# Decoder layer on one core: cross attention, routing and shared expert joined into one stage

## Chip, cores and metric

The kernel runs on one core of a Trainium2 chip. The metric is the device time of one execution in microseconds (us). Engines are named as in the profile: PE is the matrix engine, PEld its weight load, DVE the vector engine, ACT the scalar engine, POOL the GpSimd engine, SP the queue that issues most DMAs.

## What is computed

One decoder layer on 16 sequences of 128 tokens with 256 features (x is 2048 x 256), in float32. Three blocks follow each other, each with a residual sum and a layer norm:

```
x = layernorm(x + self_attention(x))                 # 16 heads of 128, 4 key/value heads
x = layernorm(x + cross(x, ctx))                     # cross:
    A = max(|sum over the batch of (x Wh)(ctx Wh)^T * decay|, 1);  O = A (ctx Wh)
    cross = (relu(x wg) * (normalised O * gamma + beta)) wo
x = layernorm(x + ffn(x))                            # ffn:
    scores = softmax(x gate^T), 64 routes;  keep the 6 largest of a token, 0 elsewhere
    flat = kept scores in 8 groups of 8;  share = sum of a group
    soft = softmax within each group, over its nonzero entries alone
    ffn = sum over 8 experts of share_f * expert_f(x, soft_f) + shared expert(x)
```

The shared expert is silu(x Wg) * (x Wu), times Wd, with 352 inner features padded to 3 tiles of 128.

## The kernel before, in words

The program is written by hand, engine by engine: every engine has its own list of instructions, and semaphores order them. There are four stages, each a block that ends with all engines meeting and the stage's semaphores cleared (L80 to L85): `self_attention` (L88), `cross_attention` (L593), `route_and_share` (L1068) and `experts` (L1377). Most products are split in a high and a low part and made of three matmuls (`product`, L45; its matmuls are L48 to L50). `keep_busy` (L53, matmul L57) multiplies an identity matrix for no result, where PE would otherwise have nothing to do.

**Self attention** works through eight turns of two sequences. In the first turn PE makes the scores of the second group of heads (L302), turns the first probabilities (L356) and then projects the next queries.

**Cross attention** works in chunks of 512 tokens, four of them (CHUNKS). For each, PE makes the mixed values (`mix_values`, L757, matmul L763), the gates (`gates`, L767, matmul L774), turns the gated values (L800), multiplies them by wo (L816) and turns the normalised result (`turn_x2`, L778, transposes L711). DVE measures the mix (`mix_factors`, L936), multiplies gate and mix (L959), adds to the residual r (`add_output`, L967), and normalises half of its tiles (L904); ACT normalises the mix (L847) and the other half (L856), and moves the turned tiles to SBUF (L863); DVE makes their low part (L991). POOL applies gamma and beta to the mix along the tokens (`affine`, L665 and L667), splits the route weights (L692, L694) and adds high and low part of the turned x again (`whole`, L590).

**Routing and shared expert**, also per chunk: logits (L1213), softmax and top six on DVE (L1311 to L1336), the kept scores turned (L1225) and copied (L1345), regrouped by a one-hot matmul (L1232), the second softmax on DVE and ACT (L1349 to L1368), written three times side by side, turned (`soft_out`, L1202) into the banks `turned_bank` and `y_bank[1]`, copied by ACT in one instruction (L1261) and by DVE in two (L1303, L1304). The shared expert's inner part (`shared_in`, silu L1250, product L1288, high part L1256, low part on POOL L1163) and its output (`shared_out`, matmuls L48 to L50 into route_y, sum L1295) lie between. In chunk 2 POOL prepares the first expert's weights in one piece (L1153 to L1159, helpers L1038 and L1057). The stage ends after the last DMAs to `soft_dram` and of the second expert's weights have landed (L1144, L1145).

**Experts**: 8 experts by 4 chunks make 32 units, in four turns of two experts. For a unit PE makes gate and up (`gate_up`, three banks), the low-rank part of the unit before (`down_low`, L1567), and its output. ACT copies the low rows of the unit before to the front (`move_low`, L1643, instruction L1646), and PE's L1567 waits for that; then ACT makes the silu of the first tile (L1667). Once per expert ACT also writes the next expert's high weights (`weights_high`, L1654).

## Time and profile before

| what | value |
|---|---|
| three runs | 959.97 us median, 958.0 to 962.97 |
| profiled execution | 958.83 us, span from first to last instruction 957.0 us |
| mean granted clock of PE | 0.986 of full speed |
| busy share of the span | PE 93%, PEld 83%, DVE 68%, ACT 54%, POOL 39% |
| DMA | 37.99 MB, 40 GB/s over the span |
| self attention | 0 to 392.1 us |
| cross attention | 392.1 to 490.2 us |
| routing and shared expert | 490.2 to 572.5 us |
| experts and the last norm | 572.5 to 957.0 us |

A group of instructions is shown by line, engine and operation, with what it writes and reads. A row of a timeline begins with its start and its length in us from the start of the span, and in square brackets the idle time of the engine before it and what ended that. A float32 matmul is recorded as two passes.

### The profile page before, as it was taken

Reading aid. Unit: us, or ns where it says so; the run is one execution under the profiler, and the core shown is the slowest. Engines: PE = TensorE matmul, PEld = TensorE weight load, DVE = VectorE, ACT = ScalarE, POOL = GpSimd, SP = SyncE. Lnnn points to the kernel's source line nnn. Section 1 sums busy time; section 2 is a strip of 40 time slices with the busy share of each in tenths; the row PEclk is TensorE's granted clock in tenths of the full one; section 3 lists DMA queues with packets and bytes.
Section 4 is the critical chain, followed back from the end, with each engine's and each line's share of the span. In section 5 each row is a group of like instructions: output and inputs, shape, how many; then the busy total and the mean of one; then the engine's idle time right before and its main releaser. Section 6 shows DMA issues by size and latency. Waiting matters only on the chain. (4 is left out here: it accounts for less than half of the span.)

```text
span 957.0 us, 16063 instructions
## 1 busy us (share of the span) xinstructions
PE 893.1 (93%) x5722; PEld 797.4 (83%) x5722; DVE 654.1 (68%) x1345; ACT 521.2 (54%) x1230; POOL 371.0 (39%) x261
## 2 busy tenths in 40 slices
PE   5899999999999999899699888999999999999994
PEld 5799999999999998687578776888888888888884
DVE  4756565646565655557758875878887778788887
ACT  4555555646474655314434426565666565656654
POOL 0721212222131312025424424665747475656441
PEclk9999999999999999999999999999999999999997
DMA  6300000000000000400010021202111020200002
GB/s 220 103 12 23 1 22 0 22 0 22 0 22 11 0 12 1 136 1 1 1 65 7 6 75 44 92 28 86 29 79 72 37 85 26 90 24 23 23 2 88
DMA packets 16429, 37.99 MB, mean 40 GB/s; under 512 B 2048, under 2 KB 6912, under 8 KB 15232
## 3 DMA queue, kind: packets, MB, share of 16 engines
q1 hardware_dynamic: 15744, 35.29, 10.8%
q0 software_dynamic: 640, 2.10, 0.7%
q8 instruction: 28, 0.46, 0.2%
q14 instruction: 17, 0.14, 0.0%
HBM read 34.76 MB, written 2.62 MB: 39 GB/s over the span
## 5 line engine op out<-in xcount | busy, mean ns | idle before, releaser
L241 POOL TENSOR_TENSOR att_probs<-att_probs,att_share 128x512 f32<-128x512 f32 x64 | 66.5, 1041 | 191.0 <-DVE att_share L525 191.0
L1494 POOL TENSOR_TENSOR all_xT_lo<-moe_inner,all_xT_lo 128x512 fp32r<-128x512 f32 x64 | 82.7, 1292 | 87.8 <-ACT all_xT_lo L1671 84.5
L429 ACT ACTIVATE att_probs<-att_score,att_bias 128x128 f32<-128x128 f32 x256 | 90.7, 381 | 41.4 <-DVE att_bias L516 41.2
L1486 POOL TENSOR_TENSOR all_xT_hi<-moe_xe,all_xT_hi 128x1024 fp32r<-128x1024 f32 x31 | 74.5, 2405 | 64.0 <-ACT all_xT_hi L1630 63.9
L1671 ACT ACTIVATE all_xT_lo<-moe_inner 128x512 fp32r<-128x512 f32 x64 | 40.4, 631 | 85.8 <-DVE moe_inner L1742 85.8
L562 DVE SCALAR_TENSOR_TENSOR att_OT_lo<-att_mix,att_bv,att_OT_hi 128x512 fp32r<-128x512 f32 x64 | 45.8, 750 | 58.0 <-ACT att_OT_hi L467 58.0
L467 ACT ACTIVATE att_OT_hi<-att_mix,att_bv 128x512 fp32r<-128x512 f32 x64 | 43.5, 704 | 66.0 <-PE att_mix L50 66.0
L48 PE MATMUL att_proj<-att_xT_hi,att_Wq_hi 128*128 128x256 f32 x256 | 74.9, 293 | 2.1 <-DVE att_Wq_lo L490 1.3
L48 PE MATMUL att_acc<-att_Wo_hi,att_OT_hi 128*128 128x256 f32 x256 | 73.0, 285 | 1.6 <-DVE att_OT_lo L562 1.6
L50 PE MATMUL att_proj<-att_xT_hi,att_Wq_lo 128*128 128x256 f32 x256 | 72.1, 282 | 0.0
L49 PE MATMUL att_proj<-att_xT_lo,att_Wq_hi 128*128 128x256 f32 x256 | 72.0, 281 | 0.0
L49 PE MATMUL att_acc<-att_Wo_lo,att_OT_hi 128*128 128x256 f32 x256 | 72.0, 281 | 0.0
L50 PE MATMUL att_acc<-att_Wo_hi,att_OT_lo 128*128 128x256 f32 x256 | 72.0, 281 | 0.0
L302 PEld LDWEIGHTS att_score<-att_KT,att_QT 128*128 128x128 f32 x512 | 61.7, 194 | 12.2 <-issue 9.1
L302 PE MATMUL att_score<-att_KT,att_QT 128*128 128x128 f32 x512 | 64.3, 279 | 7.1 <-DVE att_QT L506 3.8
L1742 DVE TENSOR_TENSOR moe_inner<-moe_gu,moe_silu 128x512 f32<-128x512 f32 x64 | 44.0, 688 | 32.8 <-ACT moe_silu L1667 13.3
L445 ACT ACTIVATE att_PT_hi<-att_mix 128x512 fp32r<-128x512 f32 x64 | 37.9, 625 | 35.6 <-PE att_mix L356 35.4
L1704 DVE TENSOR_TENSOR moe_xe<-moe_xe,all_xT 128x512 f32<-128x512 f32 x64 | 44.3, 693 | 18.2 <-PE moe_xe L1529 17.2
L429 ACT ACTIVATION_READ_ACCUMULATOR att_probs<-att_score,att_bias 128x1 f32 x256 | 56.1, 219 | 0.0
L1752 DVE SCALAR_TENSOR_TENSOR all_r<-moe_y,moe_shares,all_r 128x256 f32<-128x256 f32 x128 | 52.8, 476 | 0.0
L48 PEld LDWEIGHTS att_proj<-att_xT_hi,att_Wq_hi 128*128 128x128 f32 x256 | 48.2, 188 | 4.0 <-ACT att_KT L419 2.4
L1667 ACT ACTIVATE moe_silu<-moe_gu 128x512 f32<-128x512 f32 x64 | 37.9, 593 | 24.1 <-PE moe_gu L50 21.1
(299 smaller groups left out, 2907.2 us busy)
## 6 DMA issues: line engine op xcount, KB each, us to landing
all_stage<-in_expert_w SPq DMA_DIRECT2D x8, 1152.0 KB, 5.1
moe_spread<-soft_dram SPq DMA_DIRECT2D x64, 128.0 KB
all_scale<-in_expert_scale SPq DMA_DIRECT2D x8, 320.0 KB, 5.3
att_xT<-in_xT SPq DMA_DIRECT2D x8, 256.0 KB, 3.1
att_stage<-in_Wq SPq DMA_DIRECT2D x4, 512.0 KB, 7.5
att_stage<-in_Wo SPq DMA_DIRECT2D x4, 512.0 KB, 6.3
att_x_tok<-in_x_tok POOLq DMA_DIRECT2D x8, 256.0 KB, 3.1
out<-all_r SPq DMA_DIRECT2D x4, 512.0 KB, 3.0
```

The lines of the kernel that those rows point to most:

```text
L48: pe.matmul(out, left.hi, right.hi, start=first, stop=False, **more)
L49: pe.matmul(out, left.hi, right.lo, start=False, stop=False, **more)
L50: return pe.matmul(out, left.lo, right.hi, start=False, stop=last, **more)
L241: pool.tensor_tensor(p3, p3, each, ALU.mult).then_inc(prob_ready, 1)
L302: mm = pe.matmul(score[b][:, h * S:(h + 1) * S], QT[j % 2][:, h * TOK + b * S:h * TOK + (b + 1) * S], KT[:, j % KV * TOK + b * S:j % KV * ...
L429: ins = act.activation(p_[:, c], score[b][:, c], ACT.Exp, bias=bias[b][:, h:h + 1], scale=SCALE, accum_out=m_[:, h:h + 1])
L562: dve.scalar_tensor_tensor(o4(OT.lo), mix[b][:, :].rearrange("p (h q) -> p h q", h=G), bv[:, j:j + 1], o4(OT.hi).bitcast(F32), ALU.add, AL ...
L1486: pool.tensor_tensor(xe[u % 2].lo[:, :], xe32[:, :], xe[u % 2].hi[:, :].bitcast(F32), ALU.subtract).then_inc(xe_lo, 1)
L1494: pool.tensor_tensor(innerT[u % 2].lo[at], inner[at], innerT[u % 2].hi[at].bitcast(F32), ALU.subtract).then_inc(inner_lo, 1)
L1704: dve.tensor_tensor(xe32[:, k * CT:(k + 1) * CT], xe_bank[:, :], xT32[:, k * B * S + c * CT:k * B * S + (c + 1) * CT], ALU.add).then_inc(x ...
L1742: dve.tensor_tensor(inner[rows, cols], up, silu[rows, cols], ALU.mult).then_inc(inner_ready, 1)
L1752: dve.scalar_tensor_tensor(here, y_bank[t // 2][:, t % 2 * D:(t % 2 + 1) * D], shares[:, e * B + at:e * B + at + 1], here, ALU.mult, ALU.a ...
```

## The change

Two stages become one, `cross_and_route`; its semaphores are cleared once, at its end. In detail:

- Cross attention: gamma and beta are applied by ACT to the turned mix (`affine`), where they stand along the partitions; the mix is turned before the gate multiplies it, the gate is made turned, and DVE's product is at once the operand of wo. POOL's `affine` and ACT's copy L875 go. The first mix factors are made for 2 + 2 tiles instead of 4, the last norm for 2 + 2. PE's order is rewritten; of the `keep_busy` calls of both stages the 14 after the key/value products stay, 8 + 14 + 14 + 10 + 8 go, 5 come. The variances get their epsilon in ACT's square root.
- Seam: the shared expert of chunk 0 and its logits start before the last two tiles of cross attention are turned.
- Routing: the second softmax takes the exponential of the kept scores straight from the bank, masks it by a comparison with 0 and doesn't subtract the maximum; the sum is kept above 0.5. The result is written once, not three times, turned into `y_bank` (last chunk: the first gate and up banks), and ACT copies it three times per half, in pieces of 32 x 512 (`soft_high`). DVE's copies L1303 and L1345 go to ACT. The order of all engines' lists is rewritten.
- The first expert's weights are loaded early, and POOL prepares them in eight pieces between the low parts of the shared expert.
- The stage no longer waits for its last DMAs; the experts' queue and POOL wait for them.
- Experts: `move_low` stands behind the first silu on ACT.
- Self attention, first turn: the next queries are projected ahead of the scores.

The diff, cut to the parts that the text speaks of:

```diff
+                    if j == 0 and weights:
+                        pe.wait_ge(w_lo, j + 5)
+                        for what in step_units(j, last):
+                            projects(what)
...
-                    if j == 0 and weights:
-                        pe.wait_ge(w_lo, j + 5)
...
-                    if j != 1:
+                    if j > 1 or j == 0 and not weights:
...
+    MIX = (range(0, 2), range(2, 4), range(4, 8), range(8, 12), range(12, 16))
+    NORM = (range(0, 4), range(4, 8), range(8, 12), range(12, 14), range(14, 16))
...
+        soft_bank = lambda c, n: (y_bank if c < CHUNKS - 1 else [gate_bank[0], up_bank[0]])[n]
...
+        def mix_of(t, h=0, n=1):
+
+            at = h * 2 * HD + t % 2 * HD
+            return bank[(6 if t // CB == 1 else 0) + t // 2 % 2][:, at:at + n * HD]
...
+            sp.wait_ge(route_lo, 1)
+            load_weights(sp, a, 0, stage, scale, expert_in)
...
+                if c == CHUNKS - 2:
+                    sp.wait_ge(expert_ready, 1)
+                    load_weights(sp, a, 1, stage, scale, expert_in)
...
+                elif n < 3:
+                    if n == 1:
+                        pool.wait_ge(out_ready, 2 * CHUNKS)
+                        pool.tensor_copy(beside(dq0)[:, :, 0], down_qa(stage))
+                    pool.tensor_copy(W0.hi[:, half(n - 1)], stage[:, half(n - 1)]).then_inc(expert_hi, 1)
+                elif n < 7:
+                    at = quarter(n - 3)
+                    pool.wait_ge(expert_hi, 2)
+                    pool.tensor_tensor(W0.lo[:, at], stage[:, at], W0.hi[:, at].bitcast(F32), ALU.subtract
...
+            for c in range(CHUNKS - 1):
+                whole_x2(c)
+            for u in range(CHUNKS * SI):
+                low_inner(u)
+                if u == 1:
+                    whole_x2(CHUNKS - 1)
+                if 2 <= u < 10:
+                    first_expert(u - 2)
...
+            def turn_mix(c):
+                for i in range(2):
+                    pe.wait_ge(y_ready, 2 * c + i + 1)
+                    if c >= 2:
...
+                    pe.wait_ge(yt_out, min(2 * (c + 1) + i + 1, 2 * CHUNKS))
...
-            gates(0, (0,))
-            pe.wait_ge(at_ready, 1)
-            mix_values(0)
-            gates(0, (1,))
-            mix_values(1)
-            keep_busy(pe, bank[4], ident, 8)
-            mix_values(2)
-            keep_busy(pe, bank[4], ident, 14)
...
+            pe.wait_ge(at_ready, 1)
+            mix_values(0)
+            mix_values(1)
+            gates(0)
+            keep_busy(pe, bank[4], ident, 5)
+            for c in range(CHUNKS):
+                turn_mix(c)
+                if c < CHUNKS - 2:
+                    mix_values(c + 2)
+                if c:
+                    turn_x2(c - 1)
+                outputs(c)
+                if c < CHUNKS - 1:
+                    gates(c + 1)
...
-            keep_busy(pe, bank[0], ident, 14)
...
+            def soft_out(c):
+                pe.wait_ge(soft2_ready, c + 1)
+                for n in range(GROUPS):
+                    if c < CHUNKS - 1:
+                        pe.wait_ge(share_added, 2 * c + n + 1)
+                    else:
+                        pe.wait_ge(inner_ready, SI * CHUNKS - 1)
+                    for t in range(TT):
+                        at = (t * GROUPS + n) * GR
+                        mm = pe.transpose(soft_bank(c, n)[0:GR, t * P:(t + 1) * P], soft2[:, at:at + GR], ident[:, :])
+                    mm.then_inc(soft_turned, 1)
...
+            shared_in(0, 0)
+            logits(0)
+            shared_in(0, 1)
...
             turn_x2(CHUNKS - 1)
-            keep_busy(pe, bank[0], ident, 10)
+            shared_in(0, 2)
+            for c in range(CHUNKS):
+                if c < CHUNKS - 1:
+                    shared_in(c + 1, 0)
+                turn_kept(c)
+                if c < CHUNKS - 1:
+                    shared_in(c + 1, 1)
+                flat(c)
+                if c == CHUNKS - 2:
+                    logits(c + 1)
+                shared_out(c)
+                if c < CHUNKS - 2:
+                    logits(c + 1)
+                if c < CHUNKS - 1:
+                    shared_in(c + 1, 2)
+                    soft_out(c)
 
...
-            keep_busy(pe, token_bank, ident, 8)
...
+            def affine(c):
+
+                if c == 0:
+                    act.wait_ge(const_in, 48)
+                for i in range(2):
+                    act.wait_ge(y_turned, 2 * c + i + 1)
+                    if c:
+                        act.wait_ge(wyt_out, 2 * (c - 1) + i + 1)
+                    for k in range(DK):
+                        at = slice(k * 2 * P, (k + 1) * 2 * P)
+                        ins = act.activation(YT[i][:, at], bank[4 + i][:, at], ACT.Identity, bias=beta[:, k:k + 1],
+                                             scale=gamma[:, k:k + 1])
+                    ins.then_inc(yt_out, 1)
...
+            for n in range(3):
+                normalise_mix(n)
             for c in range(CHUNKS):
-                for i in range(2):
-                    act.wait_ge(wyt_ready, 2 * c + i + 1)
-                    act.activation(WYT[i][:, :], bank[4 + i][:, :], ACT.Copy).then_inc(wyt_out, 1)
                 if c:
                     deviation(c - 1)
+                affine(c)
...
+            def soft_high(c):
+                for n in range(GROUPS):
+                    act.wait_ge(soft_turned, GROUPS * c + n + 1)
+                    for at in (0, 2 * GR):
+                        ins = act.activation(softT[n][at:at + GR, c * CT:(c + 1) * CT], soft_bank(c, n)[0:GR, :], ACT.Copy)
+                    if c:
+                        act.wait_ge(soft_stored, 16 * GROUPS * c)
+                    act.activation(softT32[:, n * CT:(n + 1) * CT], soft_bank(c, n)[0:GR, :], ACT.Copy
+                                   ).then_inc(softT32_ready, 1)
...
+            for c in range(CHUNKS):
+                if c < CHUNKS - 1:
+                    shared(c + 1, 0)
+                take_kept(c)
+                if c < CHUNKS - 1:
+                    shared(c + 1, 1)
+                exp2(c)
+                if c < CHUNKS - 1:
+                    exp1(c + 1)
+                    shared(c + 1, 2)
+                soft_high(c)
...
-                dve.wait_ge(top2_ready, n)
-                dve.tensor_tensor(e2_8, e2_8, wide(top2, TT * F, F), ALU.subtract).then_inc(less2_ready, 1)
-                dve.wait_ge(exp2_ready, n)
+
+                dve.scalar_tensor_tensor(e2[:, :], token_bank[:, 0:TT * FK], 0.0, e2[:, :], ALU.is_gt, ALU.mult
+                                         ).then_inc(masked_ready2, 1)
+
+            def soften(c):
+                n = c + 1
+                dve.wait_ge(masked_ready2, n)
                 dve.tensor_reduce(mass2[:, :], e2_8, AX.X, ALU.add).then_inc(mass2_ready, 1)
                 dve.wait_ge(mass2_ready, n)
+                dve.tensor_scalar(mass2[:, :], mass2[:, :], 0.5, None, ALU.max).then_inc(guard_ready, 1)
+                dve.wait_ge(guard_ready, n)
                 dve.reciprocal(part2[:, :], mass2[:, :]).then_inc(part2_ready, 1)
                 dve.wait_ge(part2_ready, n)
-                four = lambda t: t.rearrange("p (t f k) -> p t f k", t=TT * GROUPS, f=F // GROUPS)
...
-                for copy in range(3):
-                    to = soft2[:, :].rearrange("p (t n c) -> p n t c", t=TT * GROUPS, n=3)[:, copy]
-                    ins = dve.tensor_tensor(to.rearrange("p t (f k) -> p t f k", k=F), four(e2[:, :]),
-                                            four(part2[:, :]).to_broadcast([P, TT * GROUPS, F // GROUPS, F]), ALU.mult)
-                ins.then_inc(soft2_ready, 1)
-            shared_out(CHUNKS - 2)
-            for n in range(GROUPS):
...
+                dve.tensor_tensor(soft2[:, :].rearrange("p (t k) -> p t k", k=F), e2_8, wide(part2, TT * F, F), ALU.mult
+                                  ).then_inc(soft2_ready, 1)
...
+            factors_x2(CHUNKS - 1)
+            variance(CHUNKS)
+            factors_x2(CHUNKS)
+            dve.wait_ge(sentinels, 2)
+            shared(0, 0)
+            largest1(0)
+            shared(0, 1)
+            choose(0)
+            for i in range(2):
+                split_x2(2 * (CHUNKS - 1) + i)
+            shared(0, 2)
+            for c in range(CHUNKS):
+                if c < CHUNKS - 1:
+                    shared(c + 1, 0)
+                    shared(c + 1, 1)
+                largest2(c)
+                if c == CHUNKS - 2:
+                    largest1(c + 1)
+                soften(c)
+                if c == CHUNKS - 1:
+                    shared_out(c, (0,))
+                    split_soft(c)
+                    shared_out(c, (1,))
+                else:
+                    shared_out(c)
+                    if c < CHUNKS - 2:
+                        largest1(c + 1)
+                    choose(c + 1)
+                    shared(c + 1, 2)
+                    split_soft(c)
+
...
             for c in range(CHUNKS):
+                sp.wait_ge(soft_stored, 16 * GROUPS * (c + 1))
                 load_spread(0, c)
...
-                if not first:
+                if first:
+                    pool.wait_ge(expert_in, 64)
+                else:
                     pool.wait_ge(w_in, e * 32 - 32)
...
-                    if not (first and u == 0):
-                        move_low(g, u - 1)
                     for k, n in ((0, 0), (1, 2)):
                         rows, cols = FEATURES[k]
                         act.wait_ge(gu_ready, 3 * count(g, u) + n + 1)
                         act.activation(silu[rows, cols], gu[n][rows, :], ACT.Silu).then_inc(silu_ready, 1)
+                        if k == 0 and not (first and u == 0):
+                            move_low(g, u - 1)
```

## Rows read from the trace of the kernel before

**Rows 1.** Busy time by stretch: engine busy us (x instructions), granted clock, DMA share, GB/s

```profile
423.50:490.20 66.70, 55.59 (x302) 45.70 (x301) 45.69 (x142) 26.20 (x64) 25.55 (x17) 0.97 0.00 1
490.20:572.50 82.30, 74.11 (x448) 63.12 (x448) 62.01 (x156) 33.30 (x49) 28.75 (x20) 0.96 0.13 44
600.00:930.00 330.00, 327.58 (x1769) 282.77 (x1768) 265.72 (x444) 206.12 (x307) 197.23 (x122) 1.00 0.14 50
```

**Rows 2.** The same stretches, PE and PEld, for L57 (keep_busy) alone

```profile
423.50:490.20 66.70, 10.92 (x92) 10.82 (x92) 0.97 0.00 1
490.20:572.50 82.30, 1.95 (x16) 1.87 (x16) 0.96 0.13 44
```

**Rows 3.** Timeline of PE, first turn of self attention

```profile
27.96 1.13 PE L302 MATMUL att_score<-att_KT,att_QT 128*128 128x128 f32 x8 [2.52 <-ACT att_probs L429]
...
37.46 2.02 PE L302 MATMUL att_score<-att_KT,att_QT 128*128 128x128 f32 x16 [0.31 <-issue]
```

**Rows 4.** Timeline of PE, cross attention and the seam

```profile
460.99 1.22 PE L800 MATMUL cross_bank<-all_ident,cross_WY 128*128 128x128 f32 x8 [2.93 <-DVE all_xT_lo L991]
...
476.14 1.75 PE L711 MATMUL cross_bank<-all_ident,all_r 128*128 128x128 f32 x8 [2.69 <-DVE all_r L904]
...
490.29 1.97 PE L1213 MATMUL route_token<-all_w,all_xT 128*128 128x64 f32 x16 [1.04 <-PEq L85]
```

**Rows 5.** Busy time by stretch, two short ones in which the granted clock is low

```profile
30.00:32.00 2.00, 2.00 (x12) 2.00 (x11) 1.15 (x3) 0.00 (x0) 1.92 (x3) 0.50 0.57 213
476.00:480.00 4.00, 3.86 (x14) 3.46 (x15) 1.39 (x3) 1.68 (x3) 0.67 (x1) 0.57 0.00 0
```

**Rows 6.** Groups of ACT in 423.5:490.2 and 490.2:572.5: count | busy us, mean ns

```profile
L847 ACT ACTIVATE cross_Y<-cross_bank,cross_oshift,cross_orstd 128x128 f32<-128x128 f32 x32 | 11.6, 469 | 2.3 <-DVE cross_oshift L947 2.3
...
L1256 ACT ACTIVATE route_inner_hi<-route_inner 128x512 fp32r<-128x512 f32 x12 | 7.6, 632 | 18.4 <-DVE route_inner L1288 18.4
...
L1261 ACT ACTIVATE all_softT<-route_y 96x512 fp32r<-96x512 f32 x4 | 2.4, 594 | 0.6 <-PE route_y L1202 0.6
```

**Rows 7.** Timeline of PE, one chunk of routing and the longest gap

```profile
517.87 1.10 PE L1232 MATMUL route_token<-route_onehot,route_keptT 64*128 64x64 f32 x8
...
523.25 1.89 PE L1213 MATMUL route_token<-all_w,all_xT 128*128 128x64 f32 x16
524.96 0.48 PE L48 MATMUL route_gate<-all_xT_hi,all_Wroute_hi 128*128 128x512 f32 x1
...
527.80 0.60 PE L1202 MATMUL route_turned<-all_ident,route_soft 128*96 128x128 f32 x4
...
535.06 1.03 PE L1225 MATMUL route_turned<-all_ident,route_kept 128*64 128x128 f32 x4 [3.32 <-DVE all_softT L1304]
```

**Rows 8.** Timeline of DVE: first and last step of choosing six routes, ten forms between

```profile
548.93 0.41 DVE L1319 TENSOR_REDUCE route_mass<-route_e 128x4 f32<-128x256 f32 x1
...
551.62 0.42 DVE L1336 TENSOR_TENSOR route_kept<-route_soft,route_rest 128x256 f32<-128x256 f32 x1
```

**Rows 9.** Timelines of POOL and DVE around 408 us

```profile
408.12 5.33 POOL L694 TENSOR_TENSOR all_Wroute_lo<-all_w,all_Wroute_hi 128x2432 fp32r<-128x2432 f32 x1
...
406.53 7.07 DVE L904 TENSOR_SCALAR all_r<-all_r,cross_mv,cross_rstd 128x256 f32<-128x256 f32 x2
```

**Rows 10.** Waits of PE (us in total, times, longest); timelines of ACT and PE, two units

```profile
PE moe_dlow L1567 <- ACT all_xT_lo L1646: 6.0, 8, 1.9
...
627.61 0.60 ACT L1667 ACTIVATE moe_silu<-moe_gu 128x512 f32<-128x512 f32 x1
...
629.23 0.39 PE L1567 MATMUL moe_dlow<-all_xT_lo,all_dq 128*128 128x512 f32 x1
...
685.35 0.63 ACT L1646 ACTIVATE all_xT_lo<-all_xT_lo 48x512 fp32r<-48x512 f32 x1
685.88 0.58 ACT L1667 ACTIVATE moe_silu<-moe_gu 128x512 f32<-128x512 f32 x1
...
686.03 0.50 PE L1567 MATMUL moe_dlow<-all_xT_lo,all_dq 128*128 128x512 f32 x1 [0.41 <-ACT all_xT_lo L1646]
```

More of the change, by code:

```diff
@@ new lines, in cross_and_route @@
+        e2 = m.sb("e2", TT * FK)
+        mass2, part2 = m.sb("mass2", TT * F), m.sb("part2", TT * F)
+        soft2 = m.sb("soft2", TT * FK)
+        silu = [ctxT0[:, n * CT:(n + 1) * CT] for n in range(2)]
+        inner = [m.sb(f"inner{n}", CT) for n in range(2)]
+        innerT = [[m.split(f"inner{n}_{k}", CT) for k in range(SI)] for n in range(2)]
+        bank = [m.bank(f"bank{n}") for n in range(8)]
+        gate_bank, up_bank, y_bank = [bank[0], bank[2]], [bank[1], bank[3]], [bank[4], bank[5]]
@@ L652, in cross_attention @@
         omv2 = omv[:, :].rearrange("p (t s) -> p t s", s=2)
+        span = lambda tiles: slice(tiles[0], tiles[-1] + 1)
         def kv_to(n):
@@ new lines, in shared_out @@
+            def shared_out(c):
+                pe.wait_ge(inner_lo, SI * (c + 1))
+                for i in range(2):
+                    if c == 0:
+                        pe.wait_ge(turned2_lo, 2 * CHUNKS)
+                    else:
+                        pe.wait_ge(softT_lo, GROUPS * (c - 1) + i + 1)
+                    if c == CHUNKS - 1 and i:
+                        soft_out(c)
+                    for j in range(2):
+                        t = 2 * i + j
+                        for k in range(SI):
+                            mm = product(pe, y_bank[i][:, j * D:(j + 1) * D], innerT[c % 2][k][:, t * P:(t + 1) * P],
+                                         Wd[:, k * D:(k + 1) * D], first=k == 0, last=k == SI - 1)
+                    mm.then_inc(share_y, 1)
@@ L1274, in _, with split_x2 @@
+            def split_x2(u):
+                dve.wait_ge(turned2_hi, u + 1)
+                to = lambda part: pairs(part[:, :])[:, :, 2 * u * P:(2 * u + 2) * P]
+                dve.tensor_tensor(to(xT.lo), pairs(bank[4 + u % 2][:, :]), to(xT.hi).bitcast(F32), ALU.subtract
+                                  ).then_inc(turned2_lo, 1)
+            for n in range(3):
+                mix_factors(n)
             dve.wait_ge(small_in, 32)
@@ L1380, in experts @@
+def experts(nc, a, r, stats, ident, xT, xT32, softT, share_of, soft_dram, stage, scale, W0, dq0, soft_stored, expert_in):
     m = Memory(nc, "moe")
```

812 lines of the change are left out of this document (363 added, 449 removed).

## Prediction

> **What bounds the kernel now.** I read the busy time by stretch first. In the experts PE is busy for 327.6 of 330 us, so any wait added there is paid in full [rows 1]. Cross attention from its gates on is another matter: of 66.7 us PE is busy for 55.6, of which 10.9 are `keep_busy` [rows 1, 2]; 11.1 us idle and 10.9 of filling make 22 us in which PE waits for chains on DVE, ACT and POOL. In routing PE is busy for 74.1 of 82.3 us, 2.0 of them filling [rows 1, 2]: idle 8.2 us. Then I read PE's timeline for what ended these waits: low parts and norms on DVE in cross attention [rows 4], and one gap of 3.3 us in routing, where the bank of the kept scores is still being read [rows 7]. The granted clock is the third view: after a gap of 2.7 us the stretch 476 to 480 ran at 0.57, that is near the lower level of 1.2 GHz, and so did 30 to 32 us at 0.50, behind a gap of 2.5 us [rows 3 to 5]. So an idle PE costs twice, once for the gap and once for the next 3 or 4 us.
>
> **Self attention.** The projection is put into the 2.5 us gap [rows 3], so the clock should hold. But ACT's copies and exponentials come before the next scores, which start at 37.46 [rows 3]; they take as long as ever, and start sooner only by what the turned probabilities gain, about half of gap and slow clock. Bounds: nothing, and the gap with 0.5 us of clock, 3. I take the middle, -1.5.
>
> **Cross attention.** Filling: 54 multiplications of the identity go from the two stages and 5 come. Of the 10.9 us in this stretch 5/46 would remain, 1.2, so -9.7. Idle: I walked through the new order with the durations of the rows and find PE waiting four times. First for the decay-weighted scores, four small DVE steps of 0.3 to 0.4 (an estimate from the forms of rows 8) that half a gate covered: 1.5. Then for the affine copies before the first output, four less what mixing and turning cover: 1.5. Then twice for the turn of the normalised tiles in chunks 1 and 2: from the variance on, ACT makes a short root (0.2), four affine copies and two norms of 256 columns before the second transposes can start. A copy of 256 columns is an estimate of 0.52, between the 0.47 of 128 and the 0.63 of 512 columns, and each starts 0.1 before the last ends [rows 6, 10], so 0.42: with handoffs 2.5 to 2.9, of which PE's own 0.9 us of transposes and the end of its gates hide some: 2.3 and 2.0. Together 7.3 instead of 11.1: -3.8. The slow stretch 476 to 480 (0.43 of 4 us) goes: -1.7. Sum -15.2, between -8 (the idle time stays whole, and one slow stretch with it) and -18 (the four waits halved). The barrier's gap of 1.0 at the seam [rows 4] is among the 11.1. Ahead of this stretch, POOL's split of the route weights holds a pair of DVE norms for 7.07 us [rows 9]; other DMAs now stand before it on SP, so it moves, off the norms or onto more of them: between -1.6 and +1, I take -0.8, as only one pair is left to meet by then.
>
> **Routing.** The work on PE is the same. What decides is a loop from one regrouping to the next, since ACT's six copies (`soft_high`) stand ahead of the silu, and that ahead of the copy of the kept scores, which PE waits for. Per chunk: regrouping and shared output 5.4 and logits 1.7 [rows 7]; maximum and difference 0.9 (two forms like those of rows 8) and exponential 0.4; choosing 3.1 [rows 8]; product 0.7 (an estimate, 512 columns against the 0.42 of 256 in rows 8) and high part 0.63; six copies of 0.59, starting 0.1 before the last ends, as ACT's do at 685 us [rows 6, 10]: 3.0; silu 0.6, product 0.7, high part 0.6, copy of the kept scores 0.6. That is 18.3, with ten handoffs of 0.05 18.8. DVE drops nine steps a chunk (four of the softmax, two of three writes, three copies) and gains a guard; that helps, and is in the walk. The head, to the first regrouping: five inner parts of 2.8 (524.96 to 527.80 [rows 7]), logits, 1.3 of transposes and about 2.7 us of waits, 19.7. Then three periods of 18.8, the last 0.5 longer, because the logits of chunk 3 there wait 3.5 us for the mask. The tail: regrouping 1.0, exponential and mask 1.3, second softmax 1.5, turn 0.9, six copies 3.0, subtraction and sum 1.4, barrier 1.0: 10.1. Sum 86.7, less 0.9 for the transposes counted above, 85.8 instead of 82.3: +3.5. So the long gap [rows 7] goes, and the copies take its place.
>
> The waits for DMAs left out at the end are in that walk, as it ends with the last sum. The two new waits in the experts, SP's for `soft_stored` and POOL's for `expert_in`, I cost at nothing: the second weights are requested some 10 us before the stage ends, and what is queued behind the waits, the first spread on SP and the scaling on POOL, is wanted some us into the stage. Without that cover it is a late DMA, 1 to 3 us once.
>
> **POOL and clock in the joint stage.** In the rows a DVE step whose operands all lie in SBUF stands still while POOL works [rows 9]. The Trainium skill (SBUF — State Buffer, section "SBUF: two separate sides") says why: the two share one port pair as an exclusive lock, and whoever comes second blocks for the whole instruction. The trace agrees, the 7.07 us end with POOL's 5.33. By that rule the eight pieces speak against the change, as they stand where DVE chooses and softens; by it alone the sum would be some 6 us higher.
>
> From rows: a quarter of the split is about 1.3 us (5.33 by 4), a low part 1.3; I find two or three meetings on the loop, half a piece each: +1, bounds 0 and +7. The new waits of 2 to 4.5 us will lower the clock three or four times, at 1.7 each as at 476, partly off the loop: +3, bounds 0 and +17. No filling stands before the experts any more: +0.5.
>
> **Experts.** `move_low` behind the silu is free in most units: the silu starts at 627.6 and PE wants the rows at 629.23; 0.6 and 0.63 fit [rows 10]. Seven times, after ACT has written the next expert's weights, both start late: PE already waits 0.41 at 686.03, and the silu takes 0.53 more ahead of it [rows 10]. The eight waits of 6.0 us are these seven and the tail [rows 10]. Seven times 0.53: +3.7, bounds 0 and +5.
>
> **Sum.** -1.5 -0.8 -15.2 +3.5 +1 +3 +0.5 +3.7 = -5.8, from 958.8 of the profiled execution to 953.0. The median lies 1.1 higher and the runs spread over 5 us, so I leave it at 953.0. About 0.5%, 4.8 us, is what a measurement can tell from no change: faster is below 955.2, slower above 964.8.
>
> **Rivals.**
> *Clock and experts cost nothing.* The waits are too short to lower the clock, and the silu's delay is hidden: 953 - 3 - 3.7 = 946. For it: gaps of 2.9 us at 461 left the clock alone [rows 4]. Against it: the experts have no slack [rows 1]. Chance 0.20.
> *POOL meets DVE at every step.* Six meetings of whole pieces, about +6 more: 959, no difference. For it: one such meeting cost over 6 us [rows 9]; the sentence on the port lock is this case. Against it: most of DVE's steps read PSUM. Chance 0.25.
> *The clock stays low around the loop's PE part: slower.* After each wait for the copies comes PE's longest part of the loop. If the lower level holds from the regrouping through the logits, 7.1 us double after the second regrouping, 7 around the late logits of chunk 3 and 3.2 in the last chunk, 17.3 instead of 3: 967. It decides if the granted clock is under 0.6 over those whole stretches. For it: 30 to 32 and 476 to 480 [rows 5]. Against it: both ended within 4 us of steady work. Chance 0.15.
> That the edit doesn't remove the seam or the filling can't be: both are plain in the lists.
>
> **How the numbers follow.** The forecast has 0.40, with a range of its own of 949 to 957; four fifths of that count as faster. Faster: 0.32 + 0.20 + 0.03 of the 959 case = 0.55; slower: 0.15 + 0.01; the same: 0.29. The range leaves out the slower case and the edge of the first rival: 942 to 964.
>
> **What would show it.** Right: cross attention from 423 us to its last output in about 50 us; regroupings 19 us apart with PE waiting about 2 us for ACT's copy before each; the experts some 8 to 11 us earlier; waits for `move_low` of about 0.9 in seven units. Wrong: regroupings under 17 us apart (then the copies are not the loop), waits for `move_low` unchanged, or a span of the experts that differs from before by something else than about 4 us.

## The result and the profile after

The changed kernel takes 963.42 us (median of 20 runs, 960.83 to 965.25), the kernel before 960.14 us: a ratio of 1.0035, 95% interval 1.0027 to 1.0044. It is slower by 3.3 us. That is less than the 0.5% that the forecast took as the least that can be told from no change, but the interval leaves 1 out, and the 953 us that were named lie on the other side of it. The range of 942 to 964 holds it by half a microsecond. The profiled execution took 962.99 us with a span of 961.3, 4.3 more than the 957.0 before.

Busy time by stretch, changed kernel: cross attention from its first mix to its last output, then routing and shared expert up to the experts' first matmul, then the same part of the experts as in [rows 1]. Columns as there.

```profile
423.40:475.84 52.44, 44.39 (x227) 38.39 (x227) 34.67 (x123) 27.81 (x68) 6.28 (x3) 0.97 0.00 1
475.84:572.34 96.50, 77.99 (x443) 67.95 (x441) 47.38 (x140) 47.99 (x76) 29.28 (x26) 0.88 0.06 22
600.00:930.00 330.00, 324.74 (x1746) 280.01 (x1745) 263.98 (x441) 204.14 (x303) 196.52 (x121) 1.00 0.14 50
```

Cross attention went as forecast: 52.4 us instead of the 66.7 of [rows 1]. But the next stretch takes 96.5 us where routing took 82.3, and there the granted clock is 0.88 instead of 0.96. The same stretches for the filling multiplications of L57 alone:

```profile
423.40:475.84 52.44, 1.28 (x10) 1.27 (x10) 0.97 0.00 1
475.84:572.34 96.50, 0.00 (x0) 0.00 (x0) 0.88 0.06 22
```

Timeline of PE in the changed kernel: the waits over 1.2 us from the first mix to the experts, and the first regrouping (495.44). L1049 is the regrouping, L987 the logits, L1176 ACT's copy of the kept scores.

```profile
424.73 3.72 PE L910 MATMUL cross_bank<-held_V,cross_AT 128*128 128x256 f32 x16 [1.37 <-DVE cross_AT L1251]
437.44 3.72 PE L958 MATMUL cross_bank<-all_cross_w,held_turned_mix 128*128 128x256 f32 x16 [1.82 <-DVE held_turned_mix L1278]
458.90 1.33 PE L856 MATMUL cross_bank<-all_ident,all_r 128*128 128x128 f32 x8 [2.39 <-ACT all_r L1131]
471.60 1.12 PE L856 MATMUL cross_bank<-all_ident,all_r 128*128 128x128 f32 x8 [2.12 <-ACT all_r L1131]
...
495.44 1.10 PE L1049 MATMUL cross_bank<-cross_onehot,cross_keptT 64*128 64x64 f32 x8
515.38 1.97 PE L1049 MATMUL cross_bank<-cross_onehot,cross_keptT 64*128 64x64 f32 x8 [3.16 <-ACT cross_keptT L1176]
536.91 1.10 PE L1049 MATMUL cross_bank<-cross_onehot,cross_keptT 64*128 64x64 f32 x8 [2.12 <-ACT cross_keptT L1176]
541.26 3.68 PE L987 MATMUL cross_bank<-cross_Wr,all_xT 128*128 128x64 f32 x16 [3.25 <-DVE cross_e L1390]
559.66 1.97 PE L1049 MATMUL cross_bank<-cross_onehot,cross_keptT 64*128 64x64 f32 x8 [4.46 <-ACT cross_keptT L1176]
572.34 0.76 PE L1594 MATMUL moe_xe<-all_softT,all_W_hi 96*128 96x512 f32 x1 [3.66 <-PEq L85]
```

The four waits of cross attention are those of the walk (1.5, 1.5, 2.3 and 2.0 were forecast). The regroupings stand 19.9, 21.5 and 22.8 us apart, PE waits each time for ACT's copy, and the same 8 matmuls that take 1.10 us at 536.91 take 1.97 at 515.38 and 559.66, where the granted clock is low. Busy time by stretch, around the three waits of over 3 us in the loop and at the start of the experts (the third column from the right is the granted clock):

```profile
514.00:522.00 8.00, 6.62 (x33) 6.50 (x34) 3.60 (x9) 3.89 (x6) 5.24 (x4) 0.57 0.04 10
538.00:550.00 12.00, 8.75 (x48) 8.74 (x48) 3.64 (x10) 4.00 (x5) 2.11 (x3) 0.57 0.01 1
558.00:566.00 8.00, 6.34 (x31) 6.16 (x32) 3.26 (x9) 3.26 (x5) 0.00 (x0) 0.57 0.57 205
572.00:576.00 4.00, 3.66 (x16) 3.50 (x17) 1.38 (x2) 0.00 (x1) 1.72 (x2) 0.57 0.26 86
```

Near the lower level of 1.2 GHz (0.5) for most of 8, 12 and 8 us, where [rows 5] had shown stretches of 2 to 4 us. The fall in the second stretch begins at 538.1 us, just as PE goes into the wait for the mask that ends at 541.26, so it follows the wait of 2.12 us ahead of the regrouping and not only the longer one.

### The profile page after: what moved, and what is told of

Read it like the earlier page. It is cut to its first block and busy times, and to the rows that moved or that the text cites. A ratio compares the mean times of both kernels' runs of the same rounds, so it can differ in the third digit from the quotient of the medians.

```text
span 961.3 us, 15888 instructions
## 1 busy us (share of the span) xinstructions
PE 888.6 (92%) x5640; PEld 797.9 (83%) x5640; DVE 627.4 (65%) x1312; ACT 537.8 (56%) x1261; POOL 351.8 (37%) x251
## 5 line engine op out<-in xcount | busy, mean ns | idle before, releaser
L1769 DVE TENSOR_TENSOR moe_xe<-moe_xe,all_xT 128x512 f32<-128x512 f32 x64 | 44.3, 692 | 19.9 <-PE moe_xe L1594 18.9
```

The lines of the kernel that those rows point to most:

```text
L1769: dve.tensor_tensor(xe32[:, k * CT:(k + 1) * CT], xe_bank[:, :], xT32[:, k * B * S + c * CT:k * B * S + (c + 1) * CT], ALU.add).then_inc(x ...
```

## The experiments

Two questions: where the time went that the walk had saved, and whether the low clock costs anything, since slow matmuls beside a wait are free. All ratios below are to the kernel before, run on the same chip.

**The low rows ahead of the silu again.**

```diff
                 for u in range(UNITS):
+                    if not (first and u == 0):
+                        move_low(g, u - 1)
                     for k, n in ((0, 0), (1, 2)):
...
-                        if k == 0 and not (first and u == 0):
-                            move_low(g, u - 1)
```

> The changed kernel, with the copy of the low rows ahead of the first silu on ACT again, as it was before. Theory: the change of place is paid at the first unit after each write of the next expert's weights, where PE's wait grew from 0.41 to 0.87 us; seven such waits at 0.47 give 3.3 us, so about 960.1 us (0.9966 of the changed kernel). Rival: those waits are covered a little later by a fuller buffer, so PE gains less than 1 us: 962.5 to 963.4.

Measured: 959.33 us, 0.9996 (0.9982 to 1.0011). PE's waits for the low rows, first in the changed kernel, then in this one:

```profile
PE moe_dlow L1632 <- ACT all_xT_lo L1711: 9.3, 8, 2.4
```

```profile
PE moe_dlow L1632 <- ACT all_xT_lo L1711: 6.0, 8, 1.9
```

Back to the 6.0 of [rows 10]. From the experts' first matmul to the end it is 385.73 us (956.0 - 570.27) against 388.96 (961.3 - 572.34): 3.2, where 3.3 was expected.

**Filling in the loop's waits.**

```diff
+                keep_busy(pe, token_bank, ident, (0, 12, 8, 16)[c])
                 flat(c)
                 if c == CHUNKS - 2:
+                    keep_busy(pe, turned_bank, ident, 13)
                     logits(c + 1)
...
+            keep_busy(pe, token_bank, ident, 13)
```

> The changed kernel, with keep_busy in PE's waits of the routing loop: 12, 8 and 16 multiplications ahead of the regroupings of chunks 1, 2 and 3, 13 ahead of the last logits, 13 at the end of the stage; they fill 2.8, 1.9, 3.8, 3.1 and 3.1 us of waits of 3.2, 2.1, 4.5, 3.3 and 3.7. Theory: the waits themselves stay, but the granted clock holds, so PE's work behind them is not stretched: 2.7 us in the second period, 3.7 in the third, 2 in the tail and 1.6 at the start of the experts, together about 10: 953.5 us. Rival: the loop is bound by ACT and DVE alone and the slow matmuls lie beside them: under 3 us, 960.5 to 963.4, with regroupings still 20 to 23 us apart. A third: the filling itself delays PE where a wait is shorter than taken, then slower than 963.4.

Measured: 954.99 us, 0.9958 (0.9940 to 0.9975), 8.4 us less than the changed kernel by the medians and 7.4 by the ratios, though it does more work. The same stretches as above, and the regroupings:

```profile
514.00:522.00 8.00, 7.49 (x65) 7.23 (x65) 3.81 (x10) 3.89 (x6) 5.28 (x4) 1.00 0.03 8
538.00:550.00 12.00, 11.66 (x89) 10.53 (x88) 7.45 (x27) 2.99 (x5) 0.00 (x0) 1.00 0.01 1
558.00:566.00 8.00, 6.74 (x58) 6.46 (x57) 2.72 (x5) 3.41 (x6) 0.83 (x1) 1.00 0.23 88
```

```profile
495.41 1.10 PE L1049 MATMUL cross_bank<-cross_onehot,cross_keptT 64*128 64x64 f32 x8
515.38 1.10 PE L1049 MATMUL cross_bank<-cross_onehot,cross_keptT 64*128 64x64 f32 x8 [0.51 <-ACT cross_keptT L1179]
534.27 1.10 PE L1049 MATMUL cross_bank<-cross_onehot,cross_keptT 64*128 64x64 f32 x8 [0.34 <-ACT cross_keptT L1179]
553.81 1.10 PE L1049 MATMUL cross_bank<-cross_onehot,cross_keptT 64*128 64x64 f32 x8 [0.88 <-ACT cross_keptT L1179]
565.18 0.47 PE L1597 MATMUL moe_xe<-all_softT,all_W_hi 96*128 96x512 f32 x1 [1.26 <-PEq L85]
```

The second regrouping happens to stand at 515.38 in both. From there to the experts it is 49.8 us at the full clock and 57.0 in the changed kernel: 7.2 us for the clock in the loop and the tail, and 1.1 more in the experts' first units (from their first matmul to the first wait for low rows 23.7 against 24.8 us). The first period, which had the full clock in both, is 20.0 against 19.9 us. The second and third are 18.9 and 19.5 us; forecast were 18.8 and 19.3. The rival, in which the slow matmuls lie beside the chain, falls. The 7.2 are rather too low: here the experts start 1.8 us behind the end of DVE's last sum (563.39), in the changed kernel 1.3 behind it (571.05), as the filling at the end of the stage lasts longer than that sum. So the clock cost some 7.7 us (an estimate from these times).

**The last logits in the usual place.**

```diff
                 flat(c)
-                if c == CHUNKS - 2:
-                    logits(c + 1)
                 shared_out(c)
-                if c < CHUNKS - 2:
+                if c < CHUNKS - 1:
                     logits(c + 1)
...
-                if c == CHUNKS - 2:
-                    largest1(c + 1)
                 soften(c)
...
-                    if c < CHUNKS - 2:
-                        largest1(c + 1)
+                    largest1(c + 1)
                     choose(c + 1)
```

> The changed kernel, with the logits of chunk 3 behind the shared output of chunk 2 on PE, and their maximum behind its sums on DVE, as in the other chunks. Theory: the 3.3 us in which PE waits for the mask go, with most of the low clock behind it; the third period falls from 22.8 to about 20 us, the kernel to about 960 us. Rival: the period is set by ACT's and DVE's chain, and the later logits lengthen it by as much as the wait was: 963 to 965.

Measured: 960.47 us, 0.9998 (0.9983 to 1.0014). The third period fell from 22.8 to 18.4 us (536.89 to 555.31), the experts start at 568.48 instead of 572.34. PE makes the output products while it would have waited for the mask, so their sums on DVE are done (544.6) before the maximum of chunk 3 (545.68). In the changed kernel they came behind slow logits and slow output products, the last at 550.8, and the choice of chunk 3, queued behind them on DVE, began at 551.4 instead of 547.05. Part of the gain is the clock: without the wait for the mask it falls at 538.3 us all the same, behind the regrouping's wait of 2.13 us, but that fall lasts 3.4 instead of 10.2 us. What the order is worth at the full clock, the four edits below show.

**POOL's pieces later.**

```diff
-                if 2 <= u < 10:
-                    first_expert(u - 2)
+                if u >= 5:
+                    first_expert(u - 5)
+            first_expert(7)
```

> The changed kernel, with POOL's eight pieces of the first expert begun three inner parts later, so that none runs while DVE softens chunk 0. Theory: there two DVE steps took 0.79 and 0.91 instead of 0.18 and 0.43 us, and the first period of the loop shrinks by about 1.1 us from 19.9: 962.3 us, no more than the measurement can just tell. Rival (POOL meets DVE at every step): the meetings are what stretches the loop, and moving them away takes 3 us or more: under 960.5.

Measured: 959.77 us, 1.0000 (0.9982 to 1.0019): the rival's number. But the trace gives the rival only 0.9 us of it. In the changed kernel two steps of DVE and two instructions of POOL (timelines):

```profile
500.43 0.79 DVE L1398 TENSOR_SCALAR cross_mass<-cross_mass 128x32 f32<-128x32 f32 x1
...
501.64 0.91 DVE L1404 TENSOR_TENSOR cross_soft<-cross_e,cross_part 128x256 f32<-128x256 f32 x1
...
499.89 1.28 POOL L810 TENSOR_TENSOR cross_inner_lo<-cross_inner,cross_inner_hi 128x512 fp32r<-128x512 f32 x1
...
501.12 1.14 POOL L825 CAST all_W_hi<-all_stage 128x1152 fp32r<-128x1152 f32 x1
```

and the same two steps here:

```profile
500.96 0.18 DVE L1399 TENSOR_SCALAR cross_mass<-cross_mass 128x32 f32<-128x32 f32 x1
...
501.56 0.42 DVE L1405 TENSOR_TENSOR cross_soft<-cross_e,cross_part 128x256 f32<-128x256 f32 x1
```

Each of the two ended just behind a POOL instruction, and 1.1 us went there, the first period falling from 19.9 to 19.0 us. This is the lock of the forecast (the Trainium skill, SBUF — State Buffer, section "SBUF: two separate sides"), met once in the loop, not at every step. The rest is the clock: PE's wait at the second regrouping was 2.11 instead of 3.16 us, the clock did not fall behind it, and the second period took 19.0 instead of 21.5 us. That a wait of 2.1 us is short enough is not shown: behind the wait of the same length at the third regrouping of this execution the clock fell at 535.1, 1.1 us after its end, as PE went into the wait for the mask.

**The changed kernel again.**

> The changed kernel itself again, beside the three that follow, for their differences and for the clock. Theory: where the granted clock falls behind a wait of about 2 us is not the same in every execution; of the changed kernel's falls those behind the long waits of the loop (515, 541 and 560 us) are there again, those behind the short ones (378 and 460 us) need not be, and the time lies within 2 us of 963.4. Rival: the falls stand where they stood, all six.

Measured: 963.25 us, 1.0041 (1.0027 to 1.0055). The falls around the long waits are there again. Of the short ones, those at 378 and 460 are not, and others are, at 47 and 470 us. Two waits of this execution:

```profile
458.46 1.12 PE L856 MATMUL cross_bank<-all_ident,all_r 128*128 128x128 f32 x8 [2.40 <-ACT all_r L1131]
469.48 1.12 PE L856 MATMUL cross_bank<-all_ident,all_r 128*128 128x128 f32 x8 [2.12 <-ACT all_r L1131]
```

and the stretches behind them:

```profile
460.00:464.00 4.00, 4.00 (x21) 3.51 (x20) 3.39 (x7) 0.21 (x1) 2.35 (x1) 1.00 0.01 4
470.00:474.00 4.00, 4.00 (x14) 3.26 (x14) 1.34 (x3) 1.09 (x2) 1.86 (x1) 0.57 0.00 0
```

In the first profile it was the other way round, with the same two waits to 0.01 us.

**Four edits together** (low rows, logits, pieces, and filling of 8, 8 and 16 ahead of the regroupings and 13 at the end).

> The changed kernel with four edits: low rows ahead of the silu, logits of chunk 3 in the usual place, POOL's pieces three inner parts later, and keep_busy in the loop's waits (8, 8 and 16 ahead of the regroupings, 13 at the end). Theory: the kernel with filling alone took 955.0; from it go 3.3 for the low rows, 1.3 for the logits and 1.1 for the pieces: 949.3, about 0.989 of the kernel before. Rival: with the clock held the three edits were only worth what the clock gave by chance, and the time stays near 955 (952 to 956).

Measured: 946.98 us, 0.9869 (0.9853 to 0.9884), 2.3 under the sum; the edits don't only give what the clock gave. Its profile says where the rest lies: the third period is 16.8 us against 19.5 in the kernel with filling alone, so the order of the logits is worth 2.8 at the full clock, not 1.3; and the way from the start of cross attention to the first regrouping is 1.7 us shorter, with one fall of the clock less, which is no work of the edits.

**More filling, outside the loop.**

```diff
+                if c >= 2:
+                    pe.wait_ge(r_ready, 2 * (c - 1) + 1)
+                    keep_busy(pe, bank[6], ident, 8)
                 if c:
                     turn_x2(c - 1)
...
+                        if last and j == KV - 1 and b == 0:
+                            keep_busy(pe, score[0], ident, 4)
```

> The same four edits, and keep_busy in three waits more: 4 in the last turn of self attention, 8 ahead of the turned norms of chunks 1 and 2 in cross attention. Theory: those waits cost the clock in part of the executions, 1.6 us at 378 and 1.6 at 460; filled, the kernel takes 1 to 3 us less than the one with the four edits, some 947. Rival: the falls were an accident of one profiled execution, the median stays the same within 0.5; or the filling stands in the way, then up to 1 us slower.

Measured: 945.84 us, 0.9855 (0.9840 to 0.9871): 1.1 less, at the lower end, with intervals that overlap. In the profiles cross attention's last output starts 1.4 us earlier (469.19 against 470.60), and the low clock at 458 us is gone.

**The third copy by POOL.**

```diff
-                    for at in (0, 2 * GR):
-                        ins = act.activation(softT[n][at:at + GR, c * CT:(c + 1) * CT], soft_bank(c, n)[0:GR, :], ACT.Copy)
+                    act.activation(softT[n][0:GR, c * CT:(c + 1) * CT], soft_bank(c, n)[0:GR, :], ACT.Copy)
...
+            def third_copy(c):
+                for n in range(GROUPS):
+                    pool.wait_ge(softT32_ready, GROUPS * c + n + 1)
+                    cols = slice(c * CT, (c + 1) * CT)
+                    pool.tensor_copy(softT[n][2 * GR:3 * GR, cols], softT[n][0:GR, cols].bitcast(F32)).then_inc(third, 1)
+                    pool.wait_ge(third, GROUPS * c + n + 1)
```

> The last kernel, with the third copy of the turned softmax made by POOL instead of ACT (two of six copies a chunk), and filling of 3, 3, 12 and 12 instead of 8, 8, 16 and 13, as the waits get shorter. Theory: ACT's six copies lie in the loop from one regrouping to the next, so it shrinks by two of them, some 1.2 us, in each of three periods and in the tail: 4 to 5 us, about 942.5, with regroupings some 17 us apart. Rival: the loop is set by DVE's steps, whose two subtractions follow the copies anyway: under 1.5 us. A third: POOL's copies (some 1 us each) get in the way of the low parts, and nothing is gained.

Measured: 941.04 us, 0.9810 (0.9796 to 0.9823), 4.8 less than the kernel before it and 22 less than the changed kernel in the same comparison. ACT in the changed kernel, from one high part to the copy that PE waits for (L1182 and L1185 are the six copies):

```profile
530.29 0.63 ACT L1162 ACTIVATE cross_inner_hi<-cross_inner 128x512 fp32r<-128x512 f32 x1 [1.70 <-DVE cross_inner L1339]
530.83 1.17 ACT L1182 ACTIVATE all_softT<-cross_bank 32x512 fp32r<-32x512 f32 x2
532.01 0.59 ACT L1185 ACTIVATE all_softT<-cross_bank 32x512 f32<-32x512 f32 x1
532.51 1.17 ACT L1182 ACTIVATE all_softT<-cross_bank 32x512 fp32r<-32x512 f32 x2
533.69 0.59 ACT L1185 ACTIVATE all_softT<-cross_bank 32x512 f32<-32x512 f32 x1
...
536.28 0.57 ACT L1176 ACTIVATE cross_keptT<-cross_bank 64x512 f32<-64x512 f32 x1
```

and the regroupings, first of the kernel before it, then of the kernel with POOL's copy:

```profile
492.08 1.10 PE L1055 MATMUL cross_bank<-cross_onehot,cross_keptT 64*128 64x64 f32 x8
510.97 1.10 PE L1055 MATMUL cross_bank<-cross_onehot,cross_keptT 64*128 64x64 f32 x8 [0.34 <-ACT cross_keptT L1181]
529.88 1.10 PE L1055 MATMUL cross_bank<-cross_onehot,cross_keptT 64*128 64x64 f32 x8 [0.35 <-ACT cross_keptT L1181]
546.82 1.10 PE L1055 MATMUL cross_bank<-cross_onehot,cross_keptT 64*128 64x64 f32 x8 [0.89 <-ACT cross_keptT L1181]
```

```profile
491.81 1.10 PE L1067 MATMUL cross_bank<-cross_onehot,cross_keptT 64*128 64x64 f32 x8
509.26 0.99 PE L1067 MATMUL cross_bank<-cross_onehot,cross_keptT 64*128 64x64 f32 x7
526.72 1.10 PE L1067 MATMUL cross_bank<-cross_onehot,cross_keptT 64*128 64x64 f32 x8
542.08 1.10 PE L1067 MATMUL cross_bank<-cross_onehot,cross_keptT 64*128 64x64 f32 x8 [0.34 <-ACT cross_keptT L1193]
```

17.5, 17.5 and 15.4 us apart, against 18.9, 18.9 and 16.9 in the kernel before it: 1.4 to 1.6 each. The smaller filling is not what shortened them, as PE waited for ACT's copy behind the larger one too. ACT's copies are in the loop. It is the fastest kernel of the study, and its filling at the end of the stage is too long: PE, DVE and PE again,

```profile
549.09 2.84 PE L57 MATMUL cross_bank<-all_ident 128*128 128x128 f32 x24
549.57 0.69 DVE L1362 TENSOR_TENSOR all_r<-cross_bank,all_r 128x512 f32<-128x512 f32 x1
553.20 0.47 PE L1607 MATMUL moe_xe<-all_softT,all_W_hi 96*128 96x512 f32 x1 [1.27 <-PEq L85]
```

The last sum ends at 550.26 and the filling at 551.93, so the stage's end waits for the filling, 1.7 us. A shorter one was not tried.

**That kernel with the old first turn of self attention** (the projection behind the turned probabilities again).

> The fastest kernel so far (four edits, filling, third copy by POOL; 941.0), with the first turn of self attention in the order of the kernel before. Theory: the projection ahead of the scores is worth 1.5 us where no fall of the clock elsewhere takes it back: 942.5, and cross attention starts at 392.1 instead of 390.5 us. Rival: it is worth nothing, 941.0 within 0.5.

Measured: 942.53 us, 0.9814 (0.9801 to 0.9828): 1.5 more by the medians, but 0.4 by the ratios, since the kernel before read 960.5 beside this run and 958.9 beside the other. By the two the size stays open. The profiles say more: cross attention starts at 391.5 to 393.0 us in the four with the old order (392.20 in the kernel before), at 390.5 to 390.7 in six of the ten with the new one, and at 392.1 to 392.5 in the other four, each of which shows a fall of the clock between 46 us and the end of the last turn.

**That kernel without the added filling.**

> The fastest kernel so far without any of the added keep_busy: the four orders and the third copy by POOL alone. Theory: the waits in cross attention (2.4 and 2.1 us), ahead of the last regrouping (3 to 4) and at the end of the stage (3.5) are open again and cost the clock 1.6, 2 and 1.6 us, with some 1 us by chance: 946 to 948; the regroupings of chunks 1 and 2, whose waits are now under 1.2 us, stay 17.5 us apart at the full clock. Rival: with the shorter loop the waits are too short for the clock to fall, and the time stays at 941 to 942.

Measured: 945.57 us, 0.9842 (0.9823 to 0.9861): 4.5 more by the medians, 3 by the ratios. The second and third regroupings stay 17.5 us apart behind waits of 0.68 us, with the clock at its full level; it falls behind the 3.0 us ahead of the last one, at the start of the experts, and twice in cross attention. The time is just under the range that was expected.

**The kernel before, filled.**

```diff
                 pe.wait_ge(wyt_out, 2 * c + 2)
+                if c >= 2:
+                    keep_busy(pe, bank[4], ident, 8)
...
+                if c == 1:
+                    keep_busy(pe, turned_bank, ident, 6)
...
                 pe.wait_ge(kept_ready, c + 1)
+                if c == 2:
+                    keep_busy(pe, token_bank, ident, 13)
```

> The kernel before, with keep_busy in those of its waits behind which the clock fell: 8 ahead of the turned norms of chunks 2 and 3 (gaps 2.3 and 2.7 us), 6 ahead of the logits of chunk 1 (1.5), 13 ahead of the turned kept scores of chunk 2 (3.3). Theory: it gains what the low clock cost in these places, 1.7 at 476, 1.7 at 508 and 1.3 at 536 us, at most 4.6: 0.995 to 0.997 of the kernel before; the joint stage with its clock held (0.9855) stays far ahead. Rival: filling alone is what made the filled kernels fast, and the kernel before filled comes to 0.99 or less.

Measured: 959.78 us, 0.9999 (0.9986 to 1.0012). Neither: nothing is gained. The 13 ended 1.8 us after the bank came free, so the same with 5:

> The kernel before, filled as in the run before, but with 5 instead of 13 multiplications ahead of the turned kept scores of chunk 2, where 13 ended 1.8 us behind the moment at which the bank came free. Theory: those 1.8 us come back, and with them a gain of 1 to 3 us on the kernel before: 0.997 to 0.999. Rival: the slow stretches of the kernel before lie beside waits that last anyway, so filling them gives nothing: 1.000 within 0.0013.

Measured: 959.47 us, 0.9995 (0.9977 to 1.0014): the rival's number; a gain of 1 us can't be excluded. In the profile with 5 the clock stays up in all of routing, and the stage takes 81.8 us (490.15 to 571.92) instead of 82.3: of the 3.0 us that were expected from its two slow stretches (1.7 and 1.3), 0.5 came, so the slow matmuls lay mostly beside waits. In cross attention the fall at 476 went, and another came at 462, behind a wait of 2.9 us that had left the clock alone [rows 4]. So filling is no gain by itself: it made the joint stage faster because PE's slow matmuls were in its loop.

## Why the prediction was wrong

The terms in the profiled executions (us). The stretches lie between the same matmuls in both, with one exception: the last 8 transposes of cross attention, 0.8 us of PE, now stand in routing. The forecast counted them in cross attention; counted there, the two rows read -13.5 and +13.4.

| step | forecast | measured |
|---|---|---|
| self attention | -1.5 | -0.1 |
| front of cross attention | -0.8 | -0.1 |
| cross attention | -15.2 | -14.3 |
| routing, with POOL (+1) and clock (+3) | +7.5 | +14.2 |
| experts, with their filling | +4.2 | +4.6 |
| sum | -5.8 | +4.3 |

**Cross attention** was right in its mechanism: filling 1.28 instead of 10.9 us, waits of 8.1 instead of the 7.3 forecast. The 1.7 us that are missing (-13.5 for -15.2) are a fall of the clock at 460 us, where the forecast let the one at 476 go and expected none: the turned norms at 458.90 and 471.60 lie 12.7 us apart, those of the repeated execution, in which the clock fell only behind the second, 11.0 (458.46 and 469.48). Its front gained nothing, as POOL's split still held one pair of norms, for 7.17 instead of 7.07 us.

**The loop** was right in its mechanism: the head of 19.6 us (19.7 forecast), periods of 18.9 and 19.5 at the full clock (18.8 and 19.3), PE waiting for ACT's copy each time. The first period was 20.0, with the one meeting of POOL and DVE, 1.1 us against the +1 of the forecast. The tail at the full clock was 11.4 instead of 10.1, with 0.5 of it due to the filling at its end.

**The experts** were right in their mechanism: seven waits grew by 0.47 us each (six from 0.41 to 0.87, the first from 1.90 to 2.37), 3.3 of the 3.7, as the first experiment shows. PE's L1632 waits for the copy that now stands behind the silu (changed kernel, ACT and PE):

```profile
686.96 0.58 ACT L1730 ACTIVATE moe_silu<-moe_gu 128x512 f32<-128x512 f32 x1
687.56 0.63 ACT L1711 ACTIVATE all_xT_lo<-all_xT_lo 48x512 fp32r<-48x512 f32 x1
...
688.24 0.50 PE L1632 MATMUL moe_dlow<-all_xT_lo,all_dq 128*128 128x512 f32 x1 [0.87 <-ACT all_xT_lo L1711]
```

**The step that failed** is the term of the clock: "three or four times, at 1.7 each as at 476, partly off the loop: +3". Of the 10.1 us between forecast and result, routing holds 5.9 (13.4 for 7.5), and the filled kernel shows the clock at work there for 7.2 to 7.7 instead of 3. Two things were wrong in the term. The size of a fall was taken from [rows 5], where the clock was back within 4 us of steady work; in the loop it stayed near the lower level for about 7, 10 and 7 us (0.57 over 8, 12 and 8 us is 6.9, 10.3 and 6.9 us at 0.5, if the rest was at the full clock). And "partly off the loop" had it backwards: PE's regrouping, shared output and logits are the loop's own first part. PE was busy for 5.7, 7.1 and 5.8 us of these falls, so it lost about half of that, 2.8, 3.5 and 2.9 us (an estimate); the second and third period were longer by 2.6 and 3.2 than in the filled kernel, and the tail by 1.3. So the periods were lengthened by nearly all that PE lost, and the tail by about half. What makes one fall longer than another stays open: behind 3.66 us at the start of the experts it lasted 3.4 us, behind 4.46 in the loop 6.9. The slower rival named this mechanism and its place. It gave 967 us, with 17.3 in the loop; that was too much, since the clock did come back before the end of these stretches. The truth lay between the two, and the forecast had taken the end that [rows 5] were nearest to, though those rows stood behind shorter waits. Its own sign shows the miss: the experts were to start 8 to 11 us earlier, and they start 0.3 us earlier (572.34 for 572.63).

**Self attention**: the 1.5 us are there in six of ten profiles, where cross attention starts at 390.7 or earlier. In the changed kernel's a fall of the clock in the last turn, at 378, behind a wait of 1.15 us that is as long in the kernel before, took them back. That this happens in part of the executions was no term of the sum. With the 1.7 in cross attention and 1.1 instead of 0.5 at the start of the experts, the clock accounts for some 8 of the 10.1 us.

**The rival of POOL at every step** (959) came within 4.4 us by its number and fell by its reason: one meeting, not six. **The rival at 946** assumed a clock that holds, and experts that cost nothing; with both made so, and two orders changed, the kernel does take 947.0.

## What to carry to other kernels

When an edit takes out filling, price the clock by what stands behind each new wait: if PE's next matmuls belong to the chain that ends the next wait, half a clock there is paid nearly in full (2.6 and 3.2 us a period here), and if they stand beside a wait, it costs little (0.5 us in the routing of the kernel before). Look for the queue that closes the loop (here ACT's six copies ahead of a silu) and move copies to an idle engine: two of six were worth 4.8 us. Filling that lasts longer than the wait is paid too (0.5 and 1.7 us at the end of the stage). And an edit whose number is right can still be credited to the wrong cause, because a fall of the clock can go or come with it; the granted clock of the stretch behind belongs beside each measured gain.

## What was not expected of the hardware

- The same wait does not always lower the clock. 2.39 us at 458 did and 2.12 at 471 didn't in one execution of the changed kernel; in the next, 2.40 didn't and 2.12 did. Ahead of the regroupings, waits of 0.68 us were not followed by a fall, and those of 3.0 us or more ahead of the last one were, in all six profiles that left them unfilled. Waits of 2.1 us stood between: ahead of the third regrouping the clock fell 1.1 to 2.2 us after their end in all five profiles that have them (in four of these PE waits for the mask by then), and ahead of the second it did not, in the one profile that has such a wait there.
- Filling one wait can be followed by a fall at another: in the kernel before, filled at 476, the clock fell at 462, behind a wait of 2.9 us that had left it alone before.
- POOL copied 32 x 512 from one quarter of the partitions to another in 0.64 us (1.28 for two), ACT in 0.57.
